# Graph network on one core: in the last sum pass the gathers add into cleared buffers

## The chip, the core and the metric

The kernel runs on one core of a Trainium2 chip. The metric is the device time of one execution in microseconds (us). The kernel before took 21892.74 us, the median of 3 runs (21871.51 to 21898.5).

## The reference

Four graph layers run one after the other on 12500 nodes with 128 features and 200000 edges. Each layer normalizes the rows, applies a ReLU, gathers rows along the edges and sums them per target node. The change is in the last layer, whose sum over edges is this (N 12500, E 200000, 128 features; `edgeFeatures` has 6 columns):

```python
transformed = nodeFeatures @ W + b
edgeMsg = edgeFeatures @ We + be
messages = transformed[src] + edgeMsg
aggregated = jax.ops.segment_sum(messages, dst, num_segments=nodeFeatures.shape[0])
return jax.nn.relu(aggregated)
```

The kernel sums the rows of `nodeFeatures` per target first and multiplies by `W` afterwards. So the pass over the edges only gathers raw rows and adds them up.

## The kernel before, in words

A first stage sorts the edges by the window of 128 nodes that their target lies in, and writes them to HBM as records. The sorted records form 1664 tiles of 128 edges (`NT`), four tiles to a group (`GT`), so 416 groups (`GROUPS`). Every tile belongs to one window. Six stages follow: an attention pass, two relation passes, a sum pass over sources (`sum_pass(k, "src")`), a dense stage (`gine_end`), a sum pass over targets (`sum_pass(k, "dst")`, the last one) and the dense end (`edge_conv_end`).

In a sum pass each engine runs its own loop over the 416 groups, and semaphores tie them together:

- POOL (`gpsimd`) issues the gathers, one indirect DMA for each tile: 128 rows of 128 floats from `table_h` in HBM to the 128 partitions of `far[:, g % RING, t, :]`. The buffer `far` is a ring of 8 groups (`RING`), so from group 8 on the gathers of group g wait until the matmuls of group g - 8 are done (`s_product`).
- DVE (`vector`) makes `hot`, a 0/1 matrix of 128 edges by 128 places in the window for each tile, three groups ahead, in one instruction of 128x512. After the matmuls of a group it adds their four results into `acc`, at a window that it reads from a table in four registers.
- PE (`tensor`) multiplies `hot` by the gathered rows, one matmul for each tile, once all rows of the group have landed (`s_ring`).
- SP and ACT fetch the rows of 51 of the 1664 tiles one by one with plain DMAs into buffers of their own (`lone`), so POOL issues 1613 gathers in each sum pass. These buffers and the sum pass over sources are not touched by the change.

Each stage is a block: all engines meet at its start and at its end. In all passes the order of work on an engine is the order of the loops below, written out.

Of the kernel before, what the change touches and what calls it, by code (L numbers as in the profile page):

```python
# [23 lines left out]
RING = 8  # L24
# [4 lines left out]
GROUPS = -(-TILES // BT) * RG  # L29
# [33 lines left out]
IDX, IDX8, LOC, TYP, ONE, ATT = range(6)  # L63
# [23 lines left out]
def over(ap, m):  # L87

    return ap.unsqueeze(1).to_broadcast([ap.shape[0], m, ap.shape[1]])
# [6 lines left out]
def windows_of(e, win, first, n):  # L96

    return e.bass.values_load_multi_w_load_instructions(win[0:1, first:first + n], engines=[e.engine],
                                                        min_val=0, max_val=W, skip_runtime_bounds_check_because=
                                                        "each is a sum of W comparisons, each 0 or 1")[1]  # L100
# [6 lines left out]
def build_program(nc, a, out):  # L107
    ctx = ExitStack()
    with ctx:
        k = Kernel()  # L110
# [32 lines left out]
        k.s_par, k.s_bias, k.s_etr, k.s_et, k.s_ec, k.s_spent = (k.sem(f"s_{n}") for n in ("par", "bias", "etr", "et", "ec", "spent"))  # L143
        k.s_agg, k.s_aggt = k.sem("s_agg"), k.sem("s_aggt")
        k.s_one = k.sem("s_one")

        k.s_moved, k.s_placed = ([k.sem(f"s_{n}{i}") for i in range(NREC)] for n in ("moved", "placed"))

# [620 lines left out]
class Stream:  # L769
# [24 lines left out]

        return [t for t in range(GT) if self.fetcher(g, t) is None]

    def gather(self, e, g, table, column):
        for t in self.tiles(g):
            index = self.rows(g, column, column + 1)[:, t, :].bitcast(I32)
            e.indirect_dma_start(out=self.far[:, g % RING, t, :], out_offset=None, in_=table,  # L800
                                 in_offset=bass.IndirectOffsetOnAxis(ap=index, axis=0)).then_inc(self.k.s_ring[g % RING], 16)

    def gathered(self, g):
# [56 lines left out]
def steps(leads):  # L860

    for step in range(-max(leads), GROUPS):
        yield [step + lead if 0 <= step + lead < GROUPS else None for lead in leads]
# [831 lines left out]
def sum_pass(k, side):  # L1695
# [3 lines left out]
    with ExitStack() as ctx:  # L1699
        sb = scratch(k, ctx, f"sum_{side}")  # L1700
        lone, ids = {n: sb(f"lone_{n}", [P, 2, F]) for n in ("sync", "scalar")}, {n: sb(f"ids_{n}", [1, 2, P], I32) for n in ("sync", "scalar")}
        st = Stream(k, side, k.recs[side], sb("far", [P, RING, GT, F]), lone, ids)
        HOT = 5
        hot = sb("hot", [P, HOT, GT, P])
        win, acc, p0 = k.win[side], k.acc, k.passes * GROUPS
        sums = [k.psum[i].rearrange("p (t f) -> p t f", t=GT) for i in range(4)]
        more, n_more, n_att = k.more[side], MORE[side], ATTRS[side]
        gine = side == "src"
# [7 lines left out]
        def beside(g, step):  # L1716

            j, i = divmod(g, BESIDE)
            return j if i == step and j < len(WIN4) else None
# [35 lines left out]
        def gpsimd(e):  # L1755
            for g in range(GROUPS):
                if g % RG == 0:
                    e.wait_ge(*st.loaded(g))
                if g >= RING:
                    e.wait_ge(k.s_product, p0 + g - RING + 1)  # L1760
                st.gather(e, g, k.table_h, IDX)

        def scalar(e):
            numbered = {1: st.number_rows(e, "scalar", 1, IDX)}
# [50 lines left out]
        def vector(e):  # L1815
            spent = 0
            if not gine:
                e.wait_ge(k.s_par, pars)
                e.tensor_tensor(wc[0:1, :], wc[0:1, :], bias[:, :], ALU.add).then_inc(k.s_bias, 1)
            for g3, g0 in steps((3, 0)):  # L1820
                if g3 is not None:
                    e.wait_ge(*st.loaded(g3))
                    if g3 >= HOT:
                        e.wait_ge(k.s_product, p0 + g3 - HOT + 1)
                    e.tensor_tensor(hot[:, g3 % HOT, :, :], over(k.col[:, :], GT), st.rows(g3, LOC, LOC + 1).to_broadcast([P, GT, P]),  # L1825
                                    ALU.is_equal).then_inc(k.s_mark, 1)
                if g0 is not None:
                    at = windows_of(e, win, g0 * GT, GT)
                    e.wait_ge(k.s_product, p0 + g0 + 1)
                    for t in range(GT):  # L1830
                        e.wait_ge(k.s_sum, GT * (p0 + g0) + t)
                        if spent:
                            e.wait_ge(k.s_spent, spent)
                        e.tensor_tensor(acc[:, bass.ds(at[t], 1), :], sums[g0 % 4][:, t:t + 1, :], acc[:, bass.ds(at[t], 1), :],  # L1834
                                        ALU.add).then_inc(k.s_sum, 1)
                    j = beside(g0, 12) if gine else None
                    if j is not None:
                        w0, n = WIN4[j]
                        e.wait_ge(k.s_ec, f0 + j + 1)
                        e.wait_ge(k.s_sum, GT * (p0 + g0 + 1))  # L1840
                        e.tensor_tensor(acc[:, w0:w0 + n, :], acc[:, w0:w0 + n, :], k.psum[6 + j % 2][:, 0:n * P].rearrange("p (n f) -> p n f", f=F),
                                        ALU.add).then_inc(k.s_spent, 1)
                        spent += 1

                        if j == 0:
                            e.wait_ge(k.s_par, pars)
                        e.tensor_tensor(k.x[:, w0:w0 + n, :], k.x[:, w0:w0 + n, :], over(bias[:, :], n), ALU.add).then_inc(k.s_bias, 1)

        with k.nc.Block() as block:
            block.sync(sync)  # L1850
            block.gpsimd(gpsimd)
            block.scalar(scalar)
            block.tensor(tensor)
            block.vector(vector)
# [284 lines left out]
```

## Time and profile before

| what | value |
|---|---|
| median of 3 runs | 21892.74 us |
| span of the profiled execution, first to last instruction | 15054.0 us |
| own time of the profiled execution beside its span | not given |
| POOL busy, whole span | 11087.4 us (74%) |
| DVE busy, whole span | 9778.7 us (65%) |
| PE busy, whole span | 8740.4 us (58%) |
| last sum pass, first gather to last sum | about 12952 to 15011 us of the span |

The span covers what the profiler recorded from the first to the last instruction. The runs' median is 6838.7 us longer; no row says what lies in that part. In the rows, "issue" is time in which an engine waited for nothing that the profile shows. A POOL row of a gather is the time in which POOL makes the DMA ready, not the time of the transfer.

### The profile page before, as it was taken

How to read it: one execution, taken by the hardware profiler on the slowest of the kernel's cores; microseconds unless marked ns; L12 is line 12 of the kernel's file. 1: busy time of each engine (PE TensorE's matmuls, PEld its weight loads, DVE VectorE, ACT ScalarE, POOL GpSimd, SP SyncE). 2: the span in 40 equal slices, each digit the busy share in tenths (PEclk: the TensorE clock that was granted, in tenths of full speed). 3: DMA queues.
4: the chain of work that ended last, by engine and by line, in shares of the span. 5: the costliest groups of instructions: out<-in, count | busy, mean ns of one | idle time of the engine just before them, and what ended most of it. 6: DMA issues, size and time to landing. Idle time of an engine off the chain costs nothing. (4 is left out here: it accounts for less than half of the span.)

```text
span 15054.0 us, 271220 instructions
## 1 busy us (share of the span) xinstructions
PE 8740.4 (58%) x56159; PEld 6734.5 (45%) x56575; DVE 9778.7 (65%) x34050; ACT 2787.6 (19%) x7303; POOL 11087.4 (74%) x11347
## 2 busy tenths in 40 slices
PE   6766667777777777555555555555444444544444
PEld 2212226666666666244444444444333333433334
DVE  8877777777878778866666677777533333433334
ACT  0011114444444444421111111111100000200000
POOL 4777767777777777777777777777677777477776
PEclk8866668999999999865555555555555555655555
DMA  2011122222222222422222222222222222422222
GB/s 85 7 42 50 53 59 74 69 69 69 69 69 69 69 69 67 152 83 59 59 58 59 58 63 63 62 63 63 69 63 63 63 62 60 121 59 59 58 59 68
DMA packets 734382, 992.39 MB, mean 66 GB/s; under 512 B 271737, under 2 KB 534898, under 8 KB 732626
## 3 DMA queue, kind: packets, MB, share of 16 engines
q0 software_dynamic: 387968, 670.55, 17.1%
q1 hardware_dynamic: 324786, 301.13, 6.5%
q8 instruction: 493, 8.08, 0.2%
q14 instruction: 1135, 9.30, 0.2%
q10 hardware_dynamic: 20000, 3.33, 0.1%
HBM read 795.25 MB, written 178.86 MB: 65 GB/s over the span
## 5 line engine op out<-in xcount | busy, mean ns | idle before, releaser
L1834 DVE TENSOR_TENSOR acc<-banks,acc 128x128 f32 x3328 | 969.8, 291 | 2616.2 <-PE banks L1792 2247.3
L668 POOL DMA_INDIRECT rec_dst<-stage_dst_sort,row_dst_sort x1563 | 1575.4, 1008 | 641.1 <-issue 474.3
L800 POOL DMA_INDIRECT far_att<-table_qv,recs_att x1664 | 1636.5, 983 | 523.9 <-issue 506.8
L800 POOL DMA_INDIRECT far_sum_dst<-table_h,recs_dst x1613 | 1561.2, 968 | 584.1 <-issue 491.7
L800 POOL DMA_INDIRECT far_sum_src<-table_h,recs_src x1613 | 1572.9, 975 | 558.8 <-issue 491.6
L800 POOL DMA_INDIRECT far_rel_src<-table_xw,recs_rel_src x1638 | 1574.7, 961 | 508.7 <-issue 494.2
L800 POOL DMA_INDIRECT far_rel_dst<-table_xw,recs_rel_dst x1638 | 1561.1, 953 | 510.4 <-issue 494.5
L1622 DVE TENSOR_TENSOR acc<-banks,acc 128x128 f32 x3328 | 969.7, 291 | 1119.2 <-PE banks L1548 1002.5
L936 POOL DMA_INDIRECT rec_src<-moved_att,row_src x1248 | 1245.0, 998 | 397.3 <-issue 379.9
L1792 PE MATMUL banks<-far_sum_src,hot_sum_src 128*128 128x128 f32 x3226 | 825.1, 436 | 1214.9 <-DVE hot_sum_src L1825 831.3
L1792 PE MATMUL banks<-far_sum_dst,hot_sum_dst 128*128 128x128 f32 x3226 | 825.9, 436 | 1147.5 <-DVE hot_sum_dst L1825 899.8
L1548 PE MATMUL banks<-far_rel_dst,hot_s_rel_dst 128*128 128x128 f32 x3276 | 836.5, 436 | 916.1 <-DVE part_rel_dst L1608 484.3
L1548 PE MATMUL banks<-far_rel_src,hot_s_rel_src 128*128 128x128 f32 x3276 | 837.5, 437 | 902.1 <-issue 388.2
L1792 PEld LDWEIGHTS banks<-far_sum_src,hot_sum_src 128*128 128x128 f32 x3226 | 715.2, 326 | 1328.0 <-DVE hot_sum_src L1825 954.9
L1792 PEld LDWEIGHTS banks<-far_sum_dst,hot_sum_dst 128*128 128x128 f32 x3226 | 715.9, 326 | 1261.9 <-DVE hot_sum_dst L1825 1014.4
L1548 PEld LDWEIGHTS banks<-far_rel_dst,hot_s_rel_dst 128*128 128x128 f32 x3276 | 726.9, 326 | 1012.5 <-DVE part_rel_dst L1608 562.8
L1548 PEld LDWEIGHTS banks<-far_rel_src,hot_s_rel_src 128*128 128x128 f32 x3276 | 727.9, 327 | 998.3 <-issue 471.7
L994 PE MATMUL banks<-ident_b,s_hi_att 128*128 128x128 bf16 x6656 | 1013.8, 232 | 45.8 <-issue 28.0
L1076 DVE TENSOR_REDUCE tile_top_att<-banks 128x8 f32<-128x1024 f32 x832 | 1012.6, 1217 | 4.6 <-PE banks L994 4.6
L994 PE MATMUL banks<-ident_b,s_lo_att 128*128 128x128 bf16 x6656 | 1010.1, 232 | 0.0
L1005 PE MATMUL banks<-x,hot_t_att 128*128 x3328 | 592.1, 333 | 463.3 <-DVE qk_att L1140 461.8
L994 PEld LDWEIGHTS banks<-ident_b,s_lo_att 128*128 128x128 bf16 x6656 | 700.5, 105 | 239.6 <-issue 76.5
(343 smaller groups left out, 21302.0 us busy)
## 6 DMA issues: line engine op xcount, KB each, us to landing
lone_sync_rel_dst<-table_xw SPq DMA_DIRECT2D x3328, 0.5 KB
lone_sync_rel_src<-table_xw SPq DMA_DIRECT2D x3328, 0.5 KB
lone_sync_sum_src<-table_h SPq DMA_DIRECT2D x3328, 0.5 KB
lone_sync_sum_dst<-table_h SPq DMA_DIRECT2D x3328, 0.5 KB
lone_scalar_sum_src<-table_h ACTq DMA_DIRECT2D x3200, 0.5 KB
lone_scalar_sum_dst<-table_h ACTq DMA_DIRECT2D x3200, 0.5 KB
table_xw<-xw_rel_tables SPq DMA_DIRECT2D x98, 512.0 KB
far_att<-table_qv,recs_att POOLq DMA_INDIRECT x1664
```

The lines of the kernel that those rows point to most:

```text
L668: e.indirect_dma_start(out=flat_dst, out_offset=bass.IndirectOffsetOnAxis(ap=row["dst"][:, c + i:c + i + 1], axis=0), in_=stage["dst"][:, ...
L800: e.indirect_dma_start(out=self.far[:, g % RING, t, :], out_offset=None, in_=table, in_offset=bass.IndirectOffsetOnAxis(ap=index, axis=0)) ...
L936: e.indirect_dma_start(out=flat_src, out_offset=bass.IndirectOffsetOnAxis(ap=k.row_src[:, t:t + 1], axis=0), in_=moved[:, b, i, :], in_off ...
L994: i = e.matmul(spread[:, t, h * P:(h + 1) * P], s[:, b, c:c + 1].to_broadcast([P, P]), k.ident_b[:, :], start=False, stop=(h == H - 1 and ...
L1005: i = e.matmul(key_rows[:, t, :], hot_t[:, g4 % 4, t, :], keys[:, bass.ds(at[t], 1), :].rearrange("p a f -> p (a f)"), start=True, stop=True)
L1076: e.tensor_reduce(tile_top[:, g % 2, t:t + 2, :].rearrange("p t h -> p (t h)"), spread[:, t:t + 2, :].rearrange("p t (h n) -> p (t h) n", ...
L1548: i = e.matmul(sums[g0 % 3][:, t, :], hot_s[:, g0 % 4, t, :], st.far_rows(g0, t), start=True, stop=True)
L1622: e.tensor_tensor(acc[:, bass.ds(at[t], 1), :], sums[g0 % 3][:, t:t + 1, :], acc[:, bass.ds(at[t], 1), :], ALU.add).then_inc(k.s_sum, 1)
L1792: i = e.matmul(sums[g % 4][:, t, :], hot[:, g % HOT, t, :], st.far_rows(g, t), start=True, stop=True)
L1834: e.tensor_tensor(acc[:, bass.ds(at[t], 1), :], sums[g0 % 4][:, t:t + 1, :], acc[:, bass.ds(at[t], 1), :], ALU.add).then_inc(k.s_sum, 1)
```

## The change

In the last sum pass alone, the gathers no longer write the rows into `far` but add them to what `far` holds (`compute_op` is add in place of bypass). So every buffer of the ring must be zero before a gather. DVE clears all 8 at the start of the pass, and after the four sums of group g it clears the buffer of group g again. A new semaphore, `s_zero`, counts the cleared buffers. The gathers of group g wait for its count g + 1, from group 0 on, and no longer for the matmuls. The sum pass over sources keeps its gathers and waits.

```diff
-    def gather(self, e, g, table, column):
+    def gather(self, e, g, table, column, op=ALU.bypass):
         for t in self.tiles(g):
             index = self.rows(g, column, column + 1)[:, t, :].bitcast(I32)
-            e.indirect_dma_start(out=self.far[:, g % RING, t, :], out_offset=None, in_=table,
+            e.indirect_dma_start(out=self.far[:, g % RING, t, :], out_offset=None, in_=table, compute_op=op,
                                  in_offset=bass.IndirectOffsetOnAxis(ap=index, axis=0)).then_inc(self.k.s_ring[g % RING], 16)
...
         def gpsimd(e):
             for g in range(GROUPS):
                 if g % RG == 0:
                     e.wait_ge(*st.loaded(g))
-                if g >= RING:
-                    e.wait_ge(k.s_product, p0 + g - RING + 1)
-                st.gather(e, g, k.table_h, IDX)
+                if gine:
+                    if g >= RING:
+                        e.wait_ge(k.s_product, p0 + g - RING + 1)
+                    st.gather(e, g, k.table_h, IDX)
+                else:
+                    e.wait_ge(k.s_zero, g + 1)
+                    st.gather(e, g, k.table_h, IDX, ALU.add)
...
             if not gine:
+                for r in range(RING):
+                    e.memset(st.far[:, r, :, :], 0.0).then_inc(k.s_zero, 1)
                 e.wait_ge(k.s_par, pars)
...
+                    if not gine and g0 + RING < GROUPS:
+                        e.memset(st.far[:, g0 % RING, :, :], 0.0).then_inc(k.s_zero, 1)
```

On DVE, at the start of the last sum pass in the program before (the sums of group 0 are the four rows of L1834 with a tensor, `hot_sum_dst` is the 0/1 matrix, L98 reads the window numbers):

```order
L1819 TENSOR_TENSOR wc_sum_dst<-wc_sum_dst,bias_sum_dst 1x128 [waits s_par]
L1825 TENSOR_TENSOR hot_sum_dst<-col,recs_dst 128x512 [waits s_rec0] x4
L98 TENSOR_LOAD win_dst
L1834 ISA [waits s_sum,s_product]
L1834 TENSOR_TENSOR acc<-banks,acc 128x128
L1834 ISA [waits s_sum]
L1834 TENSOR_TENSOR acc<-banks,acc 128x128
L1834 ISA [waits s_sum]
L1834 TENSOR_TENSOR acc<-banks,acc 128x128
L1834 ISA [waits s_sum]
L1834 TENSOR_TENSOR acc<-banks,acc 128x128
L1825 TENSOR_TENSOR hot_sum_dst<-col,recs_dst 128x512 [waits s_rec1]
```

The same place of DVE in the changed program, from the start of the pass and then from the third sum of group 0 (L1824 and L1844 are the new instructions):

```order
L1824 MEMSET far_sum_dst 128x512 x8
L1826 TENSOR_TENSOR wc_sum_dst<-wc_sum_dst,bias_sum_dst 1x128 [waits s_par]
L1832 TENSOR_TENSOR hot_sum_dst<-col,recs_dst 128x512 [waits s_rec0] x4
...
L1841 ISA [waits s_sum]
L1841 TENSOR_TENSOR acc<-banks,acc 128x128
L1841 ISA [waits s_sum]
L1841 TENSOR_TENSOR acc<-banks,acc 128x128
L1844 MEMSET far_sum_dst 128x512
L1832 TENSOR_TENSOR hot_sum_dst<-col,recs_dst 128x512 [waits s_rec1]
```

Each group now has a clearing between its last sum and the next 0/1 matrix, and the pass begins with eight. On POOL, the gathers of the same stretch before (`recs_dst` holds the row numbers):

```order
L800 DMA far_sum_dst<-table_h,recs_dst 128x128 [waits s_rec0]
L800 DMA far_sum_dst<-table_h,recs_dst 128x128 x15
L800 DMA far_sum_dst<-table_h,recs_dst 128x128 [waits s_rec1]
L800 DMA far_sum_dst<-table_h,recs_dst 128x128 x15
L800 DMA far_sum_dst<-table_h,recs_dst 128x128 [waits s_product,s_rec2]
L800 DMA far_sum_dst<-table_h,recs_dst 128x128 x3
```

And in the changed program:

```order
L801 DMA far_sum_dst<-table_h,recs_dst 128x128 [waits s_zero,s_rec0]
L801 DMA far_sum_dst<-table_h,recs_dst 128x128 x3
L801 DMA far_sum_dst<-table_h,recs_dst 128x128 [waits s_zero]
L801 DMA far_sum_dst<-table_h,recs_dst 128x128 x3
L801 DMA far_sum_dst<-table_h,recs_dst 128x128 [waits s_zero]
L801 DMA far_sum_dst<-table_h,recs_dst 128x128 x3
```

The gathers stand in the same order and number; the first of each group waits for `s_zero` where from group 8 on it waited for `s_product`.

## Rows read from the trace of the kernel before

**Rows 1.** The page: busy tenths in 40 slices; the source pass's gathers.

```profile
span 15054.0 us, 271220 instructions
...
DVE  8877777777878778866666677777533333433334
ACT  0011114444444444421111111111100000200000
POOL 4777767777777777777777777777677777477776
PEclk8866668999999999865555555555555555655555
...
L800 POOL DMA_INDIRECT far_sum_src<-table_h,recs_src x1613 | 1572.9, 975 | 558.8 <-issue 491.6 <-POOLq L1687 66.6 <-PE banks L1792 0.6
```

**Rows 2.** Groups in 12950 to 15013 us: count | busy us, mean ns | idle before.

```profile
L800 POOL DMA_INDIRECT far_sum_dst<-table_h,recs_dst x1613 | 1561.2, 968 | 584.1 <-issue 491.7 <-POOLq L2034 92.0 <-PE banks L1792 0.3
L1792 PE MATMUL banks<-far_sum_dst,hot_sum_dst 128*128 128x128 f32 x3226 | 825.9, 436 | 1147.5 <-DVE hot_sum_dst L1825 899.8 <-issue 223.9 <-DMA far_sum_dst<-table_h,recs_dst 23.9
L1834 DVE TENSOR_TENSOR acc<-banks,acc 128x128 f32 x1664 | 484.9, 291 | 1317.9 <-PE banks L1792 1135.3 <-DVE acc L1834 5.4 <-issue 3.2
L1825 DVE TENSOR_TENSOR hot_sum_dst<-col,recs_dst 128x512 f32<-128x512 f32 x416 | 288.0, 693 | 0.0
```

**Rows 3.** One tile each: indirect DMAs on POOL, duration ns min/median/max, first and last start.

```profile
L800 POOL DMA_INDIRECT far_sum_dst<-table_h,recs_dst x1613: 943/947/2343, 12952.1 to 15004.4; - x180
L800 POOL DMA_INDIRECT far_att<-table_qv,recs_att x1664: 942/963/1466, 2244.3 to 6025.1; - x185
L936 POOL DMA_INDIRECT rec_src<-moved_att,row_src x1248: 957/977/1533, 2266.4 to 6028.9; - x179
```

**Rows 4.** Timeline of POOL, start of the last sum pass: start us, us, what [idle].

```profile
12952.07 0.95 POOL L800 DMA_INDIRECT far_sum_dst<-table_h,recs_dst  x1 [92.02 <-POOLq L2034]
...
12955.83 2.34 POOL L800 DMA_INDIRECT far_sum_dst<-table_h,recs_dst  x1 [0.30 <-issue]
```

**Rows 5.** Timeline of DVE, the same stretch.

```profile
12954.66 0.28 DVE L1819 TENSOR_TENSOR wc_sum_dst<-wc_sum_dst,bias_sum_dst 1x128 f32<-1x128 f32 x1 [6.43 <-DMA bias_sum_dst<-in_L_gnn_be]
12954.87 2.48 DVE L1825 TENSOR_TENSOR hot_sum_dst<-col,recs_dst 128x512 f32<-128x512 f32 x4
12961.98 1.59 DVE L1834 TENSOR_TENSOR acc<-banks,acc 128x128 f32 x4 [4.63 <-PE banks L1792]
```

**Rows 6.** The clearings on DVE of two other sizes: busy us, mean ns.

```profile
L1042 DVE MEMSET acc<- 128x13860 f32 x1 | 11.6, 11608 | 2.8 <-issue 2.8
...
L1041 DVE MEMSET top_att<- 128x396 f32 x1 | 0.4, 388 | 0.0
L1040 DVE MEMSET x<- 128x128 f32 x1 | 0.2, 165 | 0.4 <-PEq L716 0.4
```

**Rows 7.** Timelines of DVE and POOL: a long clearing and the gathers beside it.

```profile
2245.51 11.61 DVE L1042 MEMSET acc<- 128x13860 f32 x1 [2.84 <-issue]
...
2245.60 0.96 POOL L800 DMA_INDIRECT far_att<-table_qv,recs_att  x1 [0.30 <-issue]
2246.86 0.94 POOL L800 DMA_INDIRECT far_att<-table_qv,recs_att  x1 [0.30 <-issue]
2248.11 0.94 POOL L800 DMA_INDIRECT far_att<-table_qv,recs_att  x1 [0.30 <-issue]
```

**Rows 8.** DMA queues in 14000 to 14900 us: packets, MB, share of 16 engines.

```profile
q0 software_dynamic: 22542, 46.23, 19.6%
q1 hardware_dynamic: 11114, 4.90, 2.2%
```

**Rows 9.** Windows with that tile alone: engine busy (count), clock, DMA, GB/s.

```profile
14000.00:14900.00 900.00, 359.87 (x1406) 312.05 (x1407) 684.81 (x706) 0.51 0.23 59
```

More of the change, by code:

```diff
@@ L145, in build_program @@
         k.s_one = k.sem("s_one")
+        k.s_zero = k.sem("s_zero")
         k.s_moved, k.s_placed = ([k.sem(f"s_{n}{i}") for i in range(NREC)] for n in ("moved", "placed"))
```

## The prediction

> **What bounds the kernel now.** I read the page's slices first, then the groups of the last sum pass, then its timeline, then the DMA queues. The slices [rows 1] show POOL at 7 tenths in nearly every slice from the second to the last, while DVE is at 3 or 4 in the last ten and PE runs at about half its clock. So the last stage is the place to ask whether POOL sets the pace.
>
> The groups of the pass [rows 2] answer that. POOL issues 1613 gathers at a mean of 968 ns, 1561.2 us busy. Its idle time between them is 491.7 us of "issue", 0.30 us a gather, and only 0.3 us in all is put down to PE. The 92.0 us are the dense stage before the pass. The first gather starts at 12952.1 and the last at 15004.4 us [rows 3], so 1612 steps take 2052.3 us, 1.273 us each. POOL never stands still for the ring of buffers. DVE works 484.9 + 288.0 = 772.9 us in the same stretch, 37%, and sits idle 1135.3 us for PE before its sums; PE in turn stands idle 1147.5 us in front of its matmuls. PE's wait is named after `hot_sum_dst`, but that matrix is made three groups ahead, so the later arrival is the gathered rows. The chain is POOL, then the transfer, PE and DVE for the last group only.
>
> One more thing costs POOL time. The shortest gather is 943 ns, the median 947 and the mean 968 [rows 2, 3]. At the start of the pass one gather took 2.34 us from 12955.83, while DVE made four 0/1 matrices from 12954.87 to 12957.35 [rows 4, 5]: the gather ended 0.82 us behind DVE's last one. So a DVE instruction with two inputs in SBUF holds a gather up. Over the pass this is small: 1561.2 - 1613 x 0.947 = 33.7 us.
>
> The profile gives no time of the profiled execution beside its span of 15054.0 us, so I make the sum in the span and carry the difference to the median, 21892.74 - 15054.0 = 6838.7 us, over unchanged. That is an assumption: if the part outside the span also contained work on gathers, the effect would be larger than mine.
>
> **The change part by part.**
>
> *The clearings.* DVE does 8 + 408 = 416 of them, 128x512 each. No row has this size. Two sizes on the same engine took 165 ns for 128 and 388 ns for 396 elements a partition, 11608 ns for 13860 [rows 6]: 223 / 268 = 0.83 ns an element, so 165 + 384 x 0.83 = 485 ns is my estimate. That makes 416 x 0.485 = 202 us more on DVE, which rises from 773 to about 975 us of 2052. It lies inside the 1135.3 us that DVE waits for PE [rows 2]: a group takes four gathers, 5.1 us, and DVE would be busy 0.69 + 4 x 0.29 + 0.49 = 2.3 us of it. What is queued behind a clearing on DVE is the next 0/1 matrix, three groups ahead of its use, and then the read of the window numbers. I cost it at nothing. Without that cover it would be 202 us.
>
> *Does a clearing hold POOL up?* The nearest rows say no: while DVE cleared 13860 elements from 2245.51 to 2257.12, three gathers went by in 0.96, 0.94 and 0.94 us, at the usual 0.30 us apart [rows 7]. So I cost it at nothing. The clearing does move the 0/1 matrix 0.49 us later in POOL's beat. That can take away the 33.7 us above or raise them. If every matrix met the start of a gather and held it up for most of its 0.69 us, the cost would be about 416 x 0.55 = 229 us. The phase drifts already, and I take 0, with -34 and +229 us as ends.
>
> *The new wait.* Group 0 shows how early the count arrives. Its gathers begin at 12952.07 and its sums start at 12961.98 and take 1.59 us [rows 4, 5], so the buffer would be cleared at about 12964.1. The gathers of group 8 come 8 x 4 x 1.273 = 40.7 us after those of group 0, at 12992.8. The wait is met 29 us early, where before the matmul met it some 31 us early. At the start the first gather waits for the first of the eight clearings. DVE sat idle 6.43 us up to 12954.66 before its first instruction of the pass [rows 5], so the eight (3.9 us) fit there, and POOL loses at most 0.5 us. Behind POOL's waiting gather only gathers are queued. The last eight groups have no clearing, so the end of the pass has none in its path. Together +0.5 us.
>
> *The adding gather.* This is the term that decides, and no row of before shows one. What the rows bound is this. POOL's time does not follow the bytes: a gather of 1 KB rows has the same shortest time (942 ns) as one of 512 B rows (943 ns), and a scatter of 84 B rows 957 ns [rows 3]. So I take it to follow the number of rows, 128 each, and what must be written down for each row. An adding transfer has two things to read for each row, the row in HBM and the buffer in SBUF, and one to write, where a plain one has one and one. The lower end is that POOL writes nothing more: +0. The upper end is that the reading side is the whole of the 947 ns and doubles: +947 ns. Both ends have the same distance from the nearest row, the plain gather; I take the middle, +0.474 us, which is also what three entries for a row in place of two would give (947 x 3/2 = 1421 ns). 1613 x 0.474 = 764 us. The ends are 0 and 1613 x 0.947 = 1527 us. None of it can hide, since POOL sets the pace.
>
> The Trainium skill (Collectives: The Full Stack, The bandwidth ceiling: the fold count and why AG ≠ RS ≠ AR) says that an add in the DMA path needs two source reads and two read descriptors for each chunk, where a copy has one. The Trainium skill (GPSIMD Engine Reference, When to use GPSIMD) has "a pair of Q7 cores (one emitting the read descriptors, the other the write descriptors)" at this work. By these two the reading core would be the longer one, and a sum by them lies between my middle and my upper end, 764 to 1527 us; a reading that only counts the copy's transfer would give 0. No row here shows the two cores apart.
>
> *The transfer itself.* The gathers' queue took 19.6% of 16 engines in 900 us with 706 gathers [rows 8, 9]: 0.196 x 900 / 706 = 0.25 us of all engines for each gather, against a beat of 1.273 us. An adding transfer would have to take five times as long to set the pace. Landing somewhat later changes only the end of the pass, +0.5 us.
>
> The sum is 764 + 0.5 + 0.5 + 0 = +765 us: a span of 15819 us, and 21892.74 + 765 = **22658 us**. Its own range is +150 to +1550 us, 22043 to 23443.
>
> **The rivals.**
>
> *A. An adding gather costs POOL what a plain one costs.* The rows speak for it in that POOL's time is the same for very different transfers: 943, 942 and 957 ns [rows 3]. If most of the 947 ns is a fixed part for an instruction, or a slower core covers the additional entries, then nothing is left. Then the time is that of before with -34 to +100 us from the phase of the 0/1 matrices: 21893 us as the likeliest. It decides for this side at 44 / 1613 = 0.027 us a gather: below that the difference is under 0.2%, about what a measurement of this kernel can tell from no change. Faster by more than 0.2% would need a gather that is 27 ns shorter than now, or 44 us from a loss of 33.7 us, which doesn't suffice.
>
> *B. The DMA engines become the bound.* If an adding transfer goes row by row, each waiting for its read of the buffer and its write, the engines' 0.25 us a gather could grow many times. At ten times it is 2.5 us, the ring fills, POOL waits for `s_zero`, and each gather takes 2.5 instead of 1.273 us: 1613 x 1.23 = +1984 us, 23877 us. At five times it costs nothing, at twenty +6000 us. Against it speaks that the engines are 78% idle here and four rows share a packet (706 gathers x 128 rows / 22542 packets); for it, that packets may have to be cut to a row each. The Trainium skill (DMA: Bandwidth & Descriptors, Rules for kernel authors) says that the accumulate reads its destination and writes it later; that makes three accesses where there were two, and no run here shows how they overlap.
>
> *C. The clearings hold POOL up.* If an even-sized short clearing took POOL's way to SBUF where the long one did not, it would add up to 0.4 us a group, 166 us, 22059 us. Rows 7 speak against it, and I give it no chance of its own.
>
> **How the numbers follow.** The forecast 0.47, A 0.28 (with 0.03 for faster by over 0.2%), B 0.25. Faster by more than 0.2%: 0.03. Within 0.2%: 0.25. Slower: 0.47 + 0.25 = 0.72. The range reaches from A's lower end, 21860, to B at eleven times, 24300; the rest of B, some 0.12, and a little below are left out.
>
> **What would show it.** The row of the POOL gathers into `far_sum_dst` decides: a mean near 1.42 us and "issue" still 0.30 is my case; 0.95 to 0.97 us is A. B shows as idle time of POOL that is put down to DVE's clearing, with a gather's own time short, and a share of q0 near 100%. 416 DVE MEMSET rows of about 485 ns should stand there, with DVE still idle for PE more than half of the pass. The gathers of the source pass, at 975 ns [rows 1], should not move. The forecast is wrong if the gather's mean lies below 1.04 us or above 1.91 us, or if the runs' time moves otherwise than the span.

## Result and profile after

| what | before | after |
|---|---|---|
| median of 18 runs each, same chip | 21873.18 us | 21939.53 us |
| fastest and slowest of them | 21845.65 to 21917.92 | 21832.7 to 21995.51 |
| span of the profiled execution | 15054.0 us [rows 1] | 21929.0 us |
| its own time | not given | 21930.67 us |
| last sum pass, first gather to end of the last | 2053.2 us | 3250.2 us |

The ratio is 1.0023, 95% interval 1.0013 to 1.0033. That is a cost of 50 us, between 28 and 72 by the interval (the medians differ by 66 us), where 765 were forecast. The span of a timed run lies 1.7 us below its time, so there is no part of 6838.7 us outside the span. The execution whose profile stands in rows 1 to 9 was unlike the timed ones. The page of after, in the same rows as [rows 1]:

```profile
span 21929.0 us, 272054 instructions
...
DVE  4285554555555555454444455555222223222223
...
POOL 4605555555555554545555555554555553888887
...
L801 POOL DMA_INDIRECT far_sum_src<-table_h,recs_src x1613 | 1609.2, 998 | 1579.2 <-DMA recs_src<-rec_src 1026.0
```

POOL is mostly at 5 tenths in the stages that were not changed and at 8 only in the last one. The source pass shows what an ordinary execution looks like with plain gathers: 1579.2 us idle, 1026.0 of it for the records `recs_src`, where [rows 1] had 558.8 us and none for records. The groups of the last pass of after, 18630 to 21890 us, which answer to [rows 2] (count | busy us, mean ns | idle us before and what ended it):

```profile
L801 POOL DMA_INDIRECT far_sum_dst<-table_h,recs_dst x1613 | 2758.7, 1710 | 584.3 <-issue 491.5 <-DVE far_sum_dst L1824 92.8
...
L1797 PE MATMUL banks<-far_sum_dst,hot_sum_dst 128*128 128x128 f32 x3226 | 829.8, 438 | 2340.5 <-issue 2300.8 <-DMA far_sum_dst<-table_h,recs_dst 36.3 <-DVE hot_sum_dst L1832 3.4
...
L1841 DVE TENSOR_TENSOR acc<-banks,acc 128x128 f32 x1664 | 484.7, 291 | 2319.9 <-PE banks L1797 2125.5 <-issue 13.4 <-DVE acc L1841 5.9
...
L1844 DVE MEMSET far_sum_dst<- 128x512 f32 x408 | 197.9, 485 | 23.3 <-issue 0.7
```

Here POOL is as the forecast has it: it waits for nothing but "issue", 0.30 us a gather, and a gather takes 1710 ns instead of 968. The clearings take 485 ns. One row of a tile gives the spread (duration in ns min/median/max, first and last start in us):

```profile
L801 POOL DMA_INDIRECT far_sum_dst<-table_h,recs_dst x1613: 1532/1541/3190, 18632.1 to 21880.7; - x180
L801 POOL DMA_INDIRECT far_sum_src<-table_h,recs_src x1613: 948/955/1470, 15344.3 to 18447.2; - x180
```

So the gathers became 742 ns longer in the mean, 1613 x 0.742 = 1197 us, and that is just what the last pass grew against the shown profile (3250.2 - 2053.2). The runs grew by 66 us. What hid the rest had to be found in an execution of before that is like its timed runs.

The gathers of the source pass, which were not to move from 975 ns, are at 998 ns here with a median of 955; the experiment one_add below comes back to that.

### The profile page after: what moved, and what is told of

Its sections match the earlier page's. It is cut to its first block and busy times, and to the rows that moved or that the text cites. A ratio compares the mean times of both kernels' runs of the same rounds, so it can differ in the third digit from the quotient of the medians.

```text
span 21929.0 us, 272054 instructions
## 1 busy us (share of the span) xinstructions
PE 9587.5 (44%) x56575; PEld 7327.5 (33%) x56575; DVE 9930.2 (45%) x34466; ACT 2769.5 (13%) x7303; POOL 12367.0 (56%) x11347
## 5 line engine op out<-in xcount | busy, mean ns | idle before, releaser
L801 POOL DMA_INDIRECT far_sum_dst<-table_h,recs_dst x1613 | 2758.7, 1710 | 584.3 <-issue 491.5
L801 POOL DMA_INDIRECT far_sum_src<-table_h,recs_src x1613 | 1609.2, 998 | 1579.2 <-DMA recs_src<-rec_src 1026.0
L1797 PE MATMUL banks<-far_sum_src,hot_sum_src 128*128 128x128 f32 x3226 | 728.4, 398 | 2385.6 <-DMA lone_sync_sum_src<-table_h 935.3
L1797 PEld LDWEIGHTS banks<-far_sum_src,hot_sum_src 128*128 128x128 f32 x3226 | 641.6, 296 | 2471.8 <-issue 1847.5
L1036 PE MATMUL banks<-mix_att,hot_f_att 128*128 128x140 f32 x3328 | 907.1, 453 | 854.3 <-DVE acc L1072 853.7
L995 PE MATMUL banks<-ident_b,s_lo_att 128*128 128x128 bf16 x6656 | 1094.1, 232 | 297.5 <-issue 294.9
L995 PE MATMUL banks<-ident_b,s_hi_att 128*128 128x128 bf16 x6656 | 1084.8, 233 | 154.4 <-issue 151.1
L1118 DVE TENSOR_TENSOR over_top_att<-score_att,banks 128x16 f32<-128x16 f32 x416 | 71.3, 171 | 2318.8 <-remote 2306.5
L1036 PEld LDWEIGHTS banks<-mix_att,hot_f_att 128*128 128x128 f32 x3328 | 781.1, 326 | 924.7 <-DVE mix_att L1130 924.7
L1565 PE MATMUL banks<-inverse,hot_t_rel_src 128*128 x1664 | 181.1, 192 | 1563.3 <-ACT hot_t_rel_src L1539 1558.1
L1565 PE MATMUL banks<-inverse,hot_t_rel_dst 128*128 x1664 | 182.9, 191 | 1525.9 <-ACT hot_t_rel_dst L1539 1496.3
```

The source lines that it names most:

```text
L995: i = e.matmul(spread[:, t, h * P:(h + 1) * P], s[:, b, c:c + 1].to_broadcast([P, P]), k.ident_b[:, :], start=False, stop=(h == H - 1 and ...
L1036: i = e.matmul(sums[t], hot_f[:, g1 % 2, t, :], mix[:, g1 % 2, t, :], start=True, stop=True)
L1118: e.tensor_tensor(over_top[:, g1 % 2, :], score[:, g1 % 4, :], top_rows, ALU.subtract).then_inc(s_below, 1)
L1565: i = e.matmul(shares[g2 % 3][:, t, :, :].rearrange("p i r -> p (i r)"), hot_t[:, g2 % 4, t, :], k.inverse3[:, bass.ds(at[t], 1), :, :].re ...
L1797: i = e.matmul(sums[g % 4][:, t, :], hot[:, g % HOT, t, :], st.far_rows(g, t), start=True, stop=True)
```

## The experiments

The first four ran on one chip (before 21856.02 us there), the next four together with before at 21860.62, the next three at 22243.16, the last two at 22266.83. The last two groups ran on two other chips, both slower, so across groups the ratios to before are compared, not the times. Where the passes of two kernels are compared in single profiles from different chips, the text says so.

**base**: before, unchanged.

> The kernel before, unchanged, for a profile whose span agrees with its timed runs (the one shown had a span of 15054.0 us, the runs take 21873). Theory 1 (all instruction queues are held up in ordinary executions, and POOL does not set the pace of the plain last pass): span near 21870 us, the last sum pass takes about 3190 us (the changed one's 3250 less the 58 us by which it is slower), POOL's plain gathers still 947 ns each, and POOL idle for about 1000 us in the pass on something else than 'issue', as in the source pass of the changed kernel (3103 us). Rival (the long span of the changed kernel belongs to the change): span near 15054 us again, last pass 2053 us.

21903.31 us (one run), span 21901.6. The rival, that the long span belongs to the change, is out. Its last pass takes 3065.1 us, not 2053.2:

```profile
L800 POOL DMA_INDIRECT far_sum_dst<-table_h,recs_dst x1613 | 1593.6, 988 | 1563.5 <-DMA recs_dst<-rec_dst 1003.0 <-issue 458.4 <-POOLq L2034 92.0
L1825 DVE TENSOR_TENSOR hot_sum_dst<-col,recs_dst 128x512 f32<-128x512 f32 x416 | 283.7, 683 | 999.7 <-DMA recs_dst<-rec_dst 999.7
...
L1792 PE MATMUL banks<-far_sum_dst,hot_sum_dst 128*128 128x128 f32 x3226 | 733.0, 399 | 2287.1 <-DMA lone_sync_sum_dst<-table_h 926.8 <-DVE hot_sum_dst L1825 684.8 <-issue 603.5
```

POOL waits 1003.0 us for the records, in 100 waits, DVE 999.7 us for the same, and PE 926.8 us for the single rows of SP. The queue of SP says why. First base, then after, then the shown profile of before (start us, duration us, SP's queue, operation, count):

```profile
20016.11 27.33 SPq L841 DMA_DIRECT2D lone_sync_sum_dst<-table_h  x32
20043.49 0.36 SPq L779 DMA_DIRECT2D recs_dst<-rec_dst  x1
20044.78 25.90 SPq L841 DMA_DIRECT2D lone_sync_sum_dst<-table_h  x32
```

```profile
20015.23 15.95 SPq L842 DMA_DIRECT2D lone_sync_sum_dst<-table_h  x32
...
20046.35 0.36 SPq L780 DMA_DIRECT2D recs_dst<-rec_dst  x1
20047.64 15.88 SPq L842 DMA_DIRECT2D lone_sync_sum_dst<-table_h  x32
```

```profile
13007.83 16.17 SPq L841 DMA_DIRECT2D lone_sync_sum_dst<-table_h  x32
```

SP issues the 32 single rows of a block, then the load of the next records, then 32 rows again. In base each 32 take 26.8 us in the median and SP waits for nothing; in the shown profile they took 16. The difference is hold-ups: gaps of 0.68 to 0.72 us between one instruction of SP's queue and the next. There are 3 in the whole shown profile and 4009 in base, 1025 of these in the last pass. 1361 of them stand before a DMA and 1309 between two register instructions, so it is not the issuing of a DMA alone that is held up. The records come late, and POOL waits for them, here 14.35 us in front of one gather:

```profile
20016.99 1.27 POOL L800 DMA_INDIRECT far_sum_dst<-table_h,recs_dst  x1 [14.35 <-DMA recs_dst<-rec_dst]
```

So in ordinary executions SP, not POOL, sets the pace of the last pass before the change. After it, SP's 32 rows take 16 us again, no such gap is left on SP or ACT in the pass, and SP now waits 1272.1 us for PE (in total, times, longest):

```profile
SPq L780 <- PE banks L1797: 1272.1, 90, 15.9
```

In all the runs below, SP has some 1000 of these gaps in each pass with plain gathers and single rows, and none in a pass whose gathers all add or that has no single rows. The sort and the attention pass have none either, and yet take 1.56 and 1.41 times as long in base as in the shown profile; what stretches those is not known.

**plain_clear**: after, with plain gathers; the clearings and the wait for `s_zero` stay.

```diff
-                    st.gather(e, g, k.table_h, IDX, ALU.add)
+                    st.gather(e, g, k.table_h, IDX)
```

> The changed kernel with plain gathers in the last pass; the 416 clearings and the waits on s_zero stay. Theory 1: gathers back to a median of 947 ns, POOL again waits about 1000 us in the pass, time as before (21873 us) within 40 us. Rival 2 (the 50 us of the change come from the clearings and the new wait, which hold up every fourth gather, and not from the longer gather): about 21920 us, and gathers that start beside a clearing lengthened by some 0.7 us.

21950.53 us, ratio 1.0048 (1.0032 to 1.0064): a miss. The clearings and the wait alone cost 0.5%, more than the whole change. Its last pass takes 3166.1 us, 101 us more than base, with the gather unchanged (median 944 ns) and 1107.5 us of waiting for records in place of 1003.0. So most of what the clearings cost here they cost by way of the records: SP has 1127 hold-ups in the pass where base has 1025, and its 32 rows take 28.4 us in the median in place of 26.8. Why the clearings should hold SP up more, no row shows. The rival's lengthened gathers are there (26 that start in or just before a clearing with the matrix behind it) but lose only 18 us in all.

**add_noclear**: after, with the ring cleared once at the start only, and the gathers waiting for the matmuls again. It leaves out the clearing of used buffers.

```diff
-                    e.wait_ge(k.s_zero, g + 1)
+                    if g < RING:
+                        e.wait_ge(k.s_zero, g + 1)
+                    else:
+                        e.wait_ge(k.s_product, p0 + g - RING + 1)
...
-                    if not gine and g0 + RING < GROUPS:
-                        e.memset(st.far[:, g0 % RING, :, :], 0.0).then_inc(k.s_zero, 1)
```

> The changed kernel with adding gathers, but the ring is cleared only once at the start and the gathers wait for the matmuls as before: it leaves out the clearing of used buffers, so each buffer sums up what it gathers. Theory 1: gather median 1541 ns; without the clearing in front of the 0/1 matrix fewer gathers are held up (the 273 us of hold-ups in the changed kernel fall to under 80 us), so the pass falls from 3250 to about 1613 x 1.846 = 2978 to 3060 us and the kernel is faster than the one before, 21670 to 21750 us. Rival 3 (the pass is set by the hold-up of all queues and takes about 3190 us whatever POOL does): 21870 us.

21725.68 us, ratio 0.9942 (0.9919 to 0.9964), as expected. Adding gathers without the 408 clearings are *faster* than before, although each takes POOL 1541 ns in the median. The last pass, 3071.4 us, is within 7 us of base's 3065.1. The gain lies in the stages before it (below, one_add).

**add_both**: after, with adding gathers and clearings in the source pass too.

```diff
+        z0 = 0 if gine else GROUPS
...
-                if gine:
-                    if g >= RING:
-                        e.wait_ge(k.s_product, p0 + g - RING + 1)
-                    st.gather(e, g, k.table_h, IDX)
-                else:
-                    e.wait_ge(k.s_zero, g + 1)
-                    st.gather(e, g, k.table_h, IDX, ALU.add)
+                e.wait_ge(k.s_zero, z0 + g + 1)
+                st.gather(e, g, k.table_h, IDX, ALU.add)
...
+            for r in range(RING):
+                e.memset(st.far[:, r, :, :], 0.0).then_inc(k.s_zero, 1)
             if not gine:
-                for r in range(RING):
-                    e.memset(st.far[:, r, :, :], 0.0).then_inc(k.s_zero, 1)
...
-                    if not gine and g0 + RING < GROUPS:
+                    if g0 + RING < GROUPS:
```

> Adding gathers into cleared buffers in both sum passes. Theory 1: the source pass too becomes paced by POOL, 1613 x 1.846 + about 273 us = 3250 us where it took 3103, so about 21940 + 147 = 22090 us. Rival (the source pass has time to spare, as the whole kernel hardly moved): 21940 us within 40.

22019.35 us, ratio 1.0083 (1.0058 to 1.0108). The source pass went from 3103.8 us in after to 3226.8, the same kind of step as the last pass made, and close to the 3250 expected; the time is 70 us below the 22090 expected.

**add_late**: after, with the clearing of a group's buffer moved behind the next 0/1 matrix.

```diff
+                if not gine and g0 and g0 - 1 + RING < GROUPS:
+                    e.memset(st.far[:, (g0 - 1) % RING, :, :], 0.0).then_inc(k.s_zero, 1)
                 if g0 is not None:
...
-                    if not gine and g0 + RING < GROUPS:
-                        e.memset(st.far[:, g0 % RING, :, :], 0.0).then_inc(k.s_zero, 1)
```

> The changed kernel with each clearing moved on DVE from in front of the next 0/1 matrix to behind it (still before the sums of the next group). In the changed kernel 368 gathers started during a clearing with a 0/1 matrix right behind it, and each was held up 0.73 us, 269 us in all; in the kernel without these clearings the hold-ups came to 94 us. Theory 1a (a gather is held up to the end of a two-input DVE instruction, also when a clearing runs in front of that one): hold-ups fall to about 90 us, last pass 3250 - 179 = 3070 us, kernel 21939 - 179 = 21760 us, faster than the one before. Rival (a clearing of itself holds a gather up): hold-ups of about 400 x 0.4 = 160 us or more remain, pass at 3140 us or more, kernel above 21830 us.

21756.12 us, ratio 0.9958 (0.9945 to 0.9972), where 21760 were expected, with the whole computation. Same clearings, same gathers, other order: the pass takes 3056.4 us instead of 3250.2. In after, DVE and POOL between 20030 and 20042 us (duration is the second column, in brackets the idle time before):

```profile
20031.84 0.48 DVE L1844 MEMSET far_sum_dst<- 128x512 f32 x1
20032.25 0.63 DVE L1832 TENSOR_TENSOR hot_sum_dst<-col,recs_dst 128x512 f32<-128x512 f32 x1
...
20030.22 1.54 POOL L801 DMA_INDIRECT far_sum_dst<-table_h,recs_dst  x1 [0.30 <-issue]
20032.07 2.21 POOL L801 DMA_INDIRECT far_sum_dst<-table_h,recs_dst  x1 [0.30 <-issue]
```

And in add_late:

```profile
20037.06 0.68 DVE L1832 TENSOR_TENSOR hot_sum_dst<-col,recs_dst 128x512 f32<-128x512 f32 x1
20037.79 0.48 DVE L1835 MEMSET far_sum_dst<- 128x512 f32 x1
...
20037.37 1.79 POOL L801 DMA_INDIRECT far_sum_dst<-table_h,recs_dst  x1 [0.30 <-issue]
20039.46 1.54 POOL L801 DMA_INDIRECT far_sum_dst<-table_h,recs_dst  x1 [0.30 <-issue]
```

In after the gather started during the clearing, and the matrix right behind held it up by 0.67 us; in add_late one that started inside the matrix lost 0.25. Counted over the pass: in after, 368 gathers that start during a clearing with the matrix behind it (or, 8 of them, up to 55 ns before that clearing) lose 732 ns each in the mean, 269 us. In add_late, 401 held-up gathers lose 196 ns each, 79 us; in add_noclear 405 lose 231 ns each, 94 us.

Neither half does it alone. Gathers that start in a clearing without a matrix behind it lose 14 ns (4 in add_late) and nothing (23 in plain_clear, -1 ns in the mean). Gathers that start with DVE idle and have a matrix start within 0.5 us behind them lose nothing either: 246 in the shown profile and 175 in base, -1 and 0 ns in the mean. Only a gather that starts in a clearing with the matrix right behind is caught by that matrix, and nearly for the whole of it. Why the clearing makes this difference, no row shows. The pass of add_late, 3056.4 us, is 1613 x 1.846 + 79 = 3057 us, POOL's own pace; it can lie below base's 3065.1 because SP is no longer held up.

**one_add**: before, with only the last group's two gathers of the pass adding (2 of 1613), into a buffer cleared once. `gather` has the argument `op` as in the change.

```diff
-                st.gather(e, g, k.table_h, IDX)
+                last = not gine and g == GROUPS - 1
+                if last:
+                    e.wait_ge(k.s_zero, 1)
+                st.gather(e, g, k.table_h, IDX, ALU.add if last else ALU.bypass)
...
+                    if not gine and g0 + RING == GROUPS - 1:
+                        e.memset(st.far[:, g0 % RING, :, :], 0.0).then_inc(k.s_zero, 1)
```

> The kernel before with adding gathers only in the last of the 416 groups of the last pass (2 of 1613 gathers, one clearing). In the kernels with adding gathers the stages before the last pass were 136 us shorter in the profile than in the kernel before, and their plain gathers took 955 ns where they took 944 ns. Theory 2 (this comes with the adding form being in the program at all): plain gathers at 955 ns, the sort near 3165 us instead of 3243 us, the last pass still about 3065 us, kernel about 21873 - 130 = 21740 us. Rival (the difference is chance between executions, or belongs to something else in those kernels): gathers 944 ns, 21873 us within 40.

21682.05 us, ratio 0.9921 (0.9898 to 0.9944). Two adding gathers at the very end make the program 0.8% faster, where 0.6% was expected. The sort at the start, with the same instructions, took 3156.4 us against 3242.9 in base, which ran on another chip, and 3190.2 in nolone_plain (below), which ran on the same one and has no adding gather. Against base the shorter time lies in POOL's idle time for ACT's staging, base first:

```profile
L668 POOL DMA_INDIRECT rec_dst<-stage_dst_sort,row_dst_sort x1563 | 1550.1, 992 | 1831.7 <-ACT stage_dst_sort L610 1142.0 <-issue 480.3 <-DVE row_dst_sort L459 209.4
```

```profile
L669 POOL DMA_INDIRECT rec_dst<-stage_dst_sort,row_dst_sort x1563 | 1574.6, 1007 | 1720.7 <-ACT stage_dst_sort L611 1038.2 <-issue 474.1 <-DVE row_dst_sort L460 208.4
```

The scatters are 15 ns longer each, the waiting is 111 us shorter.

**nolone_plain**: before, with no single rows by SP and ACT in the last pass; POOL gathers all 1664 tiles.

```diff
-        st = Stream(k, side, k.recs[side], sb("far", [P, RING, GT, F]), lone, ids)
+        st = Stream(k, side, k.recs[side], sb("far", [P, RING, GT, F]), lone if side == "src" else None, ids)
...
-                if c:
+                if c and gine:
                     single_rows(c - 1)
-            single_rows(BLOCKS - 1)
+            if gine:
+                single_rows(BLOCKS - 1)
...
-                if s >= LONES:
+                if s >= LONES or not gine:
                     continue
```

> The kernel before, but in the last pass POOL gathers all 1664 tiles and SP and ACT fetch no single rows. This takes 6528 DMAs and some 20000 instructions of SP and ACT out of the pass. Theory 3 (the pass of 3065 us is set by a hold-up of the instruction queues that grows with the number of instructions and DMAs, 11.4 a us here): the pass falls to POOL's own pace, 1664 x 1.27 = 2115 us, kernel about 21873 - 950 = 20920 us. Rival (the hold-up has nothing to do with their number, it stretches any pass by half): 1664 x 1.27 x 1.5 = 3170 us, kernel 21980 us.

21160.51 us, ratio 0.9691 (0.9673 to 0.971). The last pass falls from 3065.1 to 2362.3 us although POOL has 51 gathers more, and no waiting for records is left. The direction was right, the size less than expected: 1664 x 1.25 would be 2080 us (2115 were expected), and the profile names 199.4 us of "remote" waits (no cause given) and 31.6 for PE:

```profile
L800 POOL DMA_INDIRECT far_sum_dst<-table_h,recs_dst x1664: 942/947/2887, 18701.7 to 21063.1; - x185
its engine sat idle before it (us, times) until:
  issue: 486.5, 1595
  remote: 199.4, 57
```

**nolone_add**: nolone_plain with the change (adding gathers, clearings, `s_zero`).

> The changed kernel, with POOL gathering all 1664 tiles of the last pass by adding gathers and no single rows. Theory 3 with theory 1: the pass is paced by POOL alone, 1664 x (1.71 + 0.305) = 3353 us, about 1240 us longer than the plain one without single rows; that is the price of the adding gather where nothing covers it, kernel about 22040 us. Rival (the adding gathers' length is partly made by the single rows' DMAs): gather median below 1.5 us.

22023.78 us, ratio 1.0081 (1.0065 to 1.0098).

```profile
L801 POOL DMA_INDIRECT far_sum_dst<-table_h,recs_dst x1664: 1532/1541/3192, 18594.2 to 21933.8; - x185
```

The pass takes 3341.2 us, 979 more than nolone_plain, where 1240 were expected; the medians differ by 863. The plain pass had 231 us of waits ("remote" and PE) that are gone here, so some of the price was still covered: 1664 x 0.594 = 988 us of longer gathers, 201 us more of hold-ups and 20 us more of "issue", less the 231.

**lone_sp_only**: before, with ACT's single rows of the last pass left to POOL, SP's kept.

```diff
-        st = Stream(k, side, k.recs[side], sb("far", [P, RING, GT, F]), lone, ids)
+        st = Stream(k, side, k.recs[side], sb("far", [P, RING, GT, F]), lone if side == "src" else {"sync": lone["sync"]}, ids)
...
-                if s >= LONES:
+                if s >= LONES or not gine:
                     continue
```

> The kernel before, but in the last pass ACT fetches no single rows (SP still does), so POOL gathers 1638 tiles. About 10000 instructions and 3200 DMAs leave the pass, half of what left in the kernel without any single rows, whose pass took 2362 us. Theory 3 (the hold-up grows with the number of instructions and DMAs in the pass): the pass falls about half way, to 2500 to 2700 us, kernel about 21300 to 21500 us. Rival (only SP's single rows matter, as POOL waits for records that SP loads between them): the pass stays above 2900 us, kernel above 21700 us.

22035.69 us, ratio 0.9903 (0.9886 to 0.9919), so the rival held and theory 3 failed. The pass takes 2946.1 us on this slower chip, POOL waits 839.8 us for records, and SP still needs 25.6 us in the median for 32 rows. Leaving out ACT's rows gains 1%, leaving out both 3% (nolone_plain): SP's own rows are the larger part of what makes the records late. No run keeps ACT's rows and leaves out SP's alone.

**nolone_all**: no single rows in the relation and the sum passes.

```diff
-        st = Stream(k, side, sb("recs", [P, NREC, BT, COLS[side]]), sb("far", [P, RING, GT, F]), lone, ids)
+        st = Stream(k, side, sb("recs", [P, NREC, BT, COLS[side]]), sb("far", [P, RING, GT, F]), None, ids)
...
-                if c:
-                    single_rows(c - 1)
-            single_rows(BLOCKS - 1)
...
```

This is the relation pass; the sum pass is cut in the same way, with ACT's rows too.

> The kernel before with no single rows fetched anywhere: POOL gathers all 1664 tiles in both relation passes and in both sum passes. Theory 3: each sum pass takes about 2360 us in place of 3065 to 3117, and each relation pass, with a quarter fewer instructions at 15.1 a us, about 2200 to 2400 us in place of 2900; kernel about 21873 - 1450 - 1100 = 19300 us. Rival (the relation passes are bound elsewhere): 20400 us.

19666.32 us, ratio 0.8841 (0.8826 to 0.8855), with the whole computation: it beats both kernels by more than 11%. The four passes take 2472.0, 2474.6, 2383.5 and 2378.4 us where base, on a faster chip, took 2901.6, 2894.8, 3116.7 and 3065.1. SP's hold-ups went from 4009 to 1. 19300 us were expected on a chip where before takes 21873; by the ratio it would be 19338 there.

**nolone_all_one**: the same with the last group's gathers adding, as in one_add.

> The kernel without any single rows, and with adding gathers in the last of the 416 groups of the last pass. Theory 2 (the adding form in the program shortens the stages before by 140 to 180 us whatever else is in it): 140 to 180 us below the same kernel without it. Rival (the gain hangs on the single rows): no difference.

19636.18 us, ratio 0.8825 (0.881 to 0.8839): 30 us below nolone_all where 140 to 180 were expected. A miss.

**one_plain** and **one_add_again**: one_add's twin, with the same wait and clearing and all gathers plain, and one_add once more.

```diff
-                st.gather(e, g, k.table_h, IDX, ALU.add if last else ALU.bypass)
+                st.gather(e, g, k.table_h, IDX)
```

> The kernel with one adding group, but that group's two gathers are plain too: one clearing and one wait on s_zero stay. Theory 2 (the adding form in the program is what made the stages before the last pass 87 us and more shorter): this one takes what the kernel before takes, within 40 us, with plain gathers at 944 to 947 ns. Rival (code moved by the few added instructions, or chance between executions): it is 100 us or more below the kernel before as well.

> The kernel with one adding group, unchanged, a second time beside its plain twin. Theory 2: again 0.6 to 0.8% below the kernel before, plain gathers 955 ns. Rival (the gain belongs to single executions or to a chip, as with the kernels without single rows, where it was 0.15%): within 0.3% of the kernel before.

22265.66 us for one_plain, ratio 0.9999 (0.999 to 1.0008), and 22201.41 for one_add_again, ratio 0.9966 (0.9954 to 0.9978). So it is the adding gather in the program, not the wait or the clearing, that shortens the stages before it: the last pass begins at 19006.1 us in place of 19055.7. The size missed: 0.6 to 0.8% were expected. One_add gained 0.8% on its chip, one_add_again 0.3% on another, and without the single rows it was 0.15%.

## Why the prediction was wrong

*"POOL never stands still", and the carried difference.* This first step failed, and the sum with it. It was true of the profile shown and of no ordinary execution. In base POOL stands still 1003.0 us in the last pass for records that SP loads too late. The 6838.7 us were not outside the span; an ordinary execution takes 1.4 to 1.6 times as long in each of its six passes, the sort counted among them (the last 3065.1 against 2053.2 us). The text named the assumption but drew from it only that the effect might be larger. Of its own signs of being wrong the last one came: the runs' time moved otherwise than the span, which went from 15054.0 to 21929.0 us.

*"None of it can hide, since POOL sets the pace."* The working of the sum failed here. 1003 us of waiting lie beside the gathers, and the longer gather uses them up. The pass of after is 1613 gathers of 1541 + 305 ns ("issue", 491.5 / 1612), 2978 us, and 269 us of hold-ups: 3247 of 3250.2 measured. Base's is 3065.1 by SP. Only 3250.2 - 3065.1 = +185 us are left of the term. With most of the cover taken away the price is there: +979 us in nolone_add.

*The size of the adding gather.* The middle between 0 and +947 ns, +474, was too low: the median rose by 1541 - 944 = 597 ns, and the mean by 742 against rows 2 (722 against base), hold-ups included. The mean of 1.71 us is inside the bounds 1.04 to 1.91 us. So where POOL does set the pace, the forecast would have been too small. The queue of the gathers shows why there is more to write down. In 20000 to 20900 us (packets, MB, share of 16 engines), base first, then after:

```profile
q0 software_dynamic: 15004, 30.76, 13.1%
```

```profile
q0 software_dynamic: 64347, 29.32, 27.1%
```

In the shown profile 22542 packets for 706 plain gathers [rows 8, 9] are 32 each. After makes a gather in 2.015 us (3250.2 / 1613), so 447 in this stretch, with 64347 / 447 = 144 packets each. The packets' sizes tell the rest: a data packet of an adding gather carries one row of 512 B, one of a plain gather 8 rows, 4096 B, and each gather has 16 small packets more (128 + 16 and 16 + 16). That is rival B's cut to a row each, and it cost POOL no wait: a gather takes 0.131 x 900 / 470 = 0.25 us of all engines in base, with 470 gathers in the stretch, and 0.271 x 900 / 447 = 0.55 us in after, twice as much and not five times. The Trainium skill (Collectives: The Full Stack, The bandwidth ceiling: the fold count and why AG ≠ RS ≠ AR) counts two reads and two read descriptors for an adding chunk; the trace agrees in direction with a factor of 1.63 in POOL's time, where the upper end of the forecast was 2. No row shows the entries themselves.

*The clearings.* 485 ns each was right to the nanosecond, and DVE had room for them: it still waits 2125.5 us for PE before its sums. That they do not hold POOL up was right of a clearing by itself and wrong of its place: right ahead of the 0/1 matrix it costs 269 us of hold-ups against 79 behind it, and the pass takes 3250.2 against 3056.4 us. The upper bound of +229 us was just exceeded: against the 33.7 us of the shown profile the hold-ups grew by 269 - 33.7 = 235 us (against the 71 us of base by 198). Rival C was given no chance of its own on the strength of a long memset without a matrix behind it [rows 7]; its effect was there, through this other mechanism, and decides whether the change is slower (after, 1.0023) or faster than before (add_late, 0.9958).

*The new wait and the transfer.* Both as forecast: POOL waits for a clearing only once, at the start, and q0 is at 27.1%, so rival B is out. Rival A was near the time, 21893 us, but not by its reason: the gather's price is real, and covered. That the time came out so near to no change is luck: +185 us in the pass and -138 before it, neither of which was in any sum.

*What was in no term.* The stages before the last pass were 137.6 us shorter in after than in base (18632.1 against 18769.7 at the first gather), and one_plain beside one_add_again shows that the adding form does this. Kernels with adding gathers reach the last pass earlier in every comparison on one chip: 18628.1 us in add_noclear against 18734.8 in plain_clear, 18585.7 in one_add against 18701.7 in nolone_plain, 17215.2 in nolone_all_one against 17233.6 in nolone_all. With +185 in the pass and -20 behind it, the two profiles differ by +27 us; the medians by +66.

*Still open.* What makes the 0.70 us hold-ups (4009 on SP and 1490 on ACT in base), and why the shown profile has 3 on SP. Why they are gone from every pass whose gathers add: 1025 on SP and 804 on ACT in the last pass of base, none in that of after, and none in either sum pass of add_both. Whether they come from the plain gathers, or only from gathers that follow each other faster, no run separates. What stretches the sort and the attention pass, which have none of them. Why plain_clear has more of them than base. Why the adding form shortens stages in which no adding gather runs, and why by so different sizes.

## What to carry to other kernels

Compare the profile's span with the timed runs first. Here they differed by a third, and the wait on which the forecast rested was not that of the timed runs; a second profile was worth more than the sum. A longer instruction costs only what its engine did not wait: look for the queue behind that wait, here a helper on SP that issues single rows between the loads, and price the helper too. And where a clearing must go between other DVE work beside gathers, try it behind the instruction that reads two inputs before you put it ahead; here the order was worth 194 us in a pass.

## What was not expected of the hardware

- An execution can differ from another of the same kernel by 6800 us in 21900, with all six passes stretched and with gaps of 0.68 to 0.72 us between instructions of SP's queue, 4009 against 3. They vanish from a pass as soon as its gathers add.
- 51 tiles fetched by SP and ACT in place of POOL cost the kernel 700 us (21860.62 against 21160.51 on one chip; the pass 3065.1 against 2362.3 on two) and save POOL 51 gathers, 51 x 1.25 = 64 us.
- A gather that adds takes POOL 1541 ns and one packet a row; a plain one takes 944 ns and has 8 rows in a data packet.
- In every program that holds even two adding gathers the plain ones take a median of 952 to 955 ns in place of 944 to 947, and yet the stages before are shorter: 18585.7 us to the last pass in one_add, 18701.7 in nolone_plain on the same chip.
- A DVE clearing of 0.48 us with a 0.63 us matrix behind it held a gather up by 0.67 us. The clearing without the matrix behind it does not (14 ns in add_late, -1 ns in plain_clear), and neither does a matrix that starts behind a gather without the clearing between (-1 ns in the shown profile).
